# Cross-attention queries as three fp32r products, fewer keys and values ahead, and shorter norm and gate chains in a two-layer decoder

## The chip, the cores and the metric

The kernel runs on one core of a Trainium2 chip. The metric is the device time of one launch in microseconds. TensorE multiplies, VectorE (DVE), ScalarE (ACT) and GpSimd (POOL) do the elementwise work, and SyncE (SP) issues most transfers.

## The reference

Input x is 16 sequences of 128 tokens by 128 channels; ctx is a second input of the same shape. Six stages follow one another, each as x + stage(layernorm(x)):

```
x = x + self_attention_0(norm(x))          # 16 heads of 8, causal
x = x + cross_attention_0(norm(x), ctx)    # 8 heads of 64, plus a bias
x = x + ternary_ffn(norm(x))               # weights in {-1,0,1}, activations rounded to 8 bits
x = x + self_attention_1(norm(x))          # 16 heads of 8, causal, scores clipped to +-10
x = x + cross_attention_1(norm(x), ctx)    # 16 heads of 64
x = x + mixture(norm(x))                   # softmax gate over 8 experts, weights under 0.1 dropped, rest renormalised
```

The norm is (x - mean) / sqrt(var + 1e-5). The query of a cross attention is norm(x) @ Wq with Wq of 128 x 512 (first) or 128 x 1024 (second); its keys and values are ctx @ Wk and ctx @ Wv. All values are fp32.

## The kernel before

**Steps and orders.** The work of one sequence is cut into named steps (`all_steps`, line 55): `cross1.q.0` is the query projection of the first eight heads of the second cross attention, `.k` and `.v` its keys and values, `.s1` the scores, `.mx` the row maxima, `.ex` the exponentials, `.rc` and `.nz` the division by the sum, `.t` and `.wT` the transpose of the weights, `.pv` the product with the values, `.y` the output projection, `.res` the residual with the statistics of the next norm. Each step belongs to one engine. Steps of several sequences are interleaved: `ORDER` holds for every engine one long written-out string, two characters to a step, that gives the order in which that engine executes all steps of all 16 sequences. Every engine runs its string in order and waits at semaphores, so a late step holds up all behind it on its engine. The class `Plan` walks through the strings with the cost of each step and assigns the eight PSUM banks; TensorE then waits for the earlier user of a bank (`room`).

**Queries.** `four_pairs` (lines 1128 to 1133) makes a query step of four fp32 matmuls: stationary a 128x128 block of Wq, moving the transposed normalised input `xnT` of 128 columns. Each has its own column block of one PSUM bank, and ScalarE copies the bank to `qT`. cross0 has one such step for each sequence, cross1 two: 48 steps in all.

**Keys, values and experts** are already computed in three products. A matrix is split into a high part (ScalarE copies it to the type fp32r, line 803) and a low part (the difference, line 590 on DVE or GpSimd), and lo x hi, hi x lo and hi x hi are added up in PSUM. Keys are made for two sequences together, so 256 columns move (lines 1226 to 1228); values move 512 columns of weights (lines 1234 to 1236), experts too (lines 1334 to 1336). Keys and values depend on ctx alone, so their steps can be put anywhere; `AHEAD` gives the number of sequences for which they are kept, 8 for cross0 and 6 for cross1.

**Norm.** DVE computes mean and variance (`bn_stats`, `bn_aggr`, lines 891 to 893). GpSimd adds eps (line 665), drains, raises to the power -1/2 (line 667), drains and multiplies by the negated mean (line 669). ScalarE normalises (line 792), TensorE transposes (line 1360) and ScalarE copies to `xnT` (line 741). For the mixture ScalarE writes the transposed input twice (lines 808 and 809) and DVE takes its low part (line 906, step `moe.xl`). In the FFN DVE clamps the scaled units in PSUM (line 912), drains and rounds them (line 916).

**Gate.** After the exponentials with their sum, DVE takes the reciprocal of the sum (line 996), scales the eight exponentials twice (lines 998, 999), compares with 0.1 and keeps (line 1001), adds 1 where nothing is kept (line 1004), takes a reciprocal (line 1006) and scales (line 1010).

Of the kernel before, what the change touches and what calls it, by code (L numbers as in the profile page):

```python
# [6 lines left out]
F32 = mybir.dt.float32  # L7
# [24 lines left out]
AHEAD = dict(cross0=8, cross1=6)  # L32
# [32 lines left out]
def all_steps():  # L65
# [8 lines left out]
    def norm(L, source, users, read="xTe"):  # L74
        add(f"{L}.rs", "POOL", 1272, [source], [f"{L}.nm"])
# [5 lines left out]
        add(f"{L}.xTe", *(("DVE", 572) if L == "ffn" else ("ACT", 332 if L == "moe" else 166)), [f"{L}.xT"])  # L81
# [37 lines left out]
    def cross_attention(L, source, chunks, following, biased, k_w, v_w, loads):  # L119
# [15 lines left out]
        fill(f"{L}.y", 893 * chunks, [f"{L}.oTe.{c}" for c in range(chunks)], f"{L}.res")  # L135
# [6 lines left out]
    for name, load, engine, hi, lo in (("ctx0", "c0", "DVE", 530, 610), ("b_k", "b_k", "DVE", 530, 610),  # L142
                                       ("b_v", "b_v", "DVE", 530, 610), ("e_k", "e_k", "POOL", 960, 2390),
# [7 lines left out]
    cross_attention("cross0", "self0.res", 1, "ffn", ["self0.bi"], "b_k", "b_v", "in.more")  # L151
# [7 lines left out]
    cross_attention("cross1", "self1.res", 2, "moe", [], "e_k", "e_v", "in.cross1")  # L159
# [6 lines left out]
    add("moe.w", "DVE", 1650, ["moe.ex"], ["moe.ml", "moe.gT"])  # L166
# [24 lines left out]
        "aZaLbycubWbYa1bSaHcGbjbUaOblbCbabYaJcKbccybGaUbEbncBaQcqbWcCchb6bebJcjcsbwcacGb8byaXclccaZaLa4a1bQa6"
        "aHcubjaObCbSaJblbGbEcyaQbnb0aUcBcKbUbacqchbcbJcsbeaXbwb6cCcaaLbyaZb8aHa1clcjccbQb2cubScGbWbUcKbjbCaO"
        "blbabEb0aJbnbccyaQaUbGcBcCb6cqb8bebJcsaXchbwcaccaZbyaLcjclcGa4a1cua6aHbjbQaOblbaaJa4bncyaQbcbSaUbCcK"
        "cBbUchbEcCcqbebJcscjaXb6bwbWcGb8aZaLcabya1bGccclaHcubjbQbYaOblbSbCb2bUbEbaaQcybncKbcchb6bGcBaUcab8be"
        "bJcjbYcqcCclcccsaXcGbwcuaJaLbybjaZbQb0b0a1blaObCaHbnbSbEa6a6aQbGcyaJbYbUcKcBaUbacCbcchcqbwb6bebJaXb8"
        "cGbycaaLcjcsccaHaZcla1cubjbYb0aOblbQb2bnbaaUcybcaQcKcBbSchaJcqbUbeaXcGcCbCcjcsaOb6aZbGb0caa1aLb8bEcK"
        "aQccbwaUclbjbycuaXbYblbJaZbab2cya1bcbncBcqbecCbCbacsbQcGbYbcchbSbEbGcKbUbjcjbJbeblb6cub8bwcaccbybWcl"
        "cybnbQb2cBbjbWcCbCbSblbEbGbUchbncqbJb6cjbwcab8cGbyclcscccubQb0b2bwbWbCbSbWcybEcKbUbGcBchcCbycjbJb6cq"
        "cab8csccclbCcubEb0bQbJbGbSbYbUchb2cGcycjb6bYcBcacqb8clcsbQcKcccGbSb0bUcucCb6b2b8cacqchcccjclcycsb0b2"
        "cBcCcKcuchcqcjcGcycscBcKcucCcGcKcycBcCcGcK"  # L200
    ),
    DVE=(
        "aEaEarataEavaPaTbpbraEaYaTaPaEa2aYaEaPaTaEbfa2bhaYaTaPa2bfboaYaEbubhbxa2aTbzaPbfboaEbhaYbubKbNa2bfbx"
        "bzbhbRaTboaPbVbubKbNbxbfbzbocdbhaYcfbRcma2bVcobubNbKbxbzcdaEbocmbRaPbVcfbuaTcocvbxaEbfbzaYbKbNbha2cm"
        "cAcDcdcocFcIcvbRaTcfaPbVcLcDbocAcFbfbucIbKaEbNbhaYbxcmcdbRbzcva2cobVaTcLaPcAcfcDbocFaEcIbubfbNbKbxbh"
        "bzaYcmcda2bRcocvcfaPaTbocAcDcLbVbucFaEbKbNbfaYbxcIbha2cmbzcdbRcocvcLcfbVaPaTboaEcAcDcFcIbubfbNbKaYbx"
        "bhcdbzcma2cfcvcobRaPaTcAbocLcDbVcFcIbubfbNbKaYbxbhbzaEcda2cmcvcfbRaPbVaTcLcAcocDbocFbfbNbubKbhcIcmcd"
        "aYbxcvbzcfbRa2coaPboaTcAbVcLcDbucFcIbxbfbNbKbzbhaYcdcma2cvcfcoaTaPbRcAcLcDbocFbVbfaYcIbhbuaPa2aTcLbx"
        "cdcmbzcfcvaYcobKa2cAbNcDbobfcFbhbRcIbVbucLbNbfbKcvbxbhcdbzcmbobRcAcDcfcocFbVcIbobubKbNbxbzcmcdbucvbR"
        "cfbxcocLcAcDbVcFcIbzbKbNcdcmcvcfbRbKbVcobNcDcFcmbRcLcdcAbVcocfcIcvcdcmcfcAcDcocLcvcFcIcDcAcFcLcvcIcA"  # L210
        "cDcFcLcIcL"
    ),
# [16 lines left out]
    POOL=(
        "apaFaFaFaNaxaSaWazaFaBaNaWaSa8aFaDaNaFaSaWa3a8biaNaFaWa3aSbsa8a3bia8aNbAaFaWaSbsbIbiaNbMbPa3bAa8aFbi"  # L230
        "bsaWb4bIaSbMbAbPbsbicga8b4cpa3aNbIbPbMbsbAaFb4cgaScpaWcwbAa3bIbMbibPaNa8aFcpcwcJcgaWb4bsaSbIbMbPbicJ"
        "bAaNa8a3cwaFb4cpbIcgbsaSaWcJbPbMbia3bAaNa8cwcpa3aFcgbsaSb4aWbIbPbMcJbibAa8aNcwaFb4cpbsaSaWbIcgcJbMbi"
        "bPa3a8bAcgcwcpaFa3aNaSbsb4aWcJbPbibIbMbAa8cwcgaFb4bscpa3bIaNaSaWbibMbPcwbAcga8a3cJbsaScpb4aNaWcJbIbi"
        "bAaNbMbPa8cwcgcpaWaSb4bscJbiaNa8a3aSaWbIbAcwcpa8bMbPcgbsbicJb4bPa3cwa3bMbIbibAbscgcpb4cJbIbsbMbPbAcw"
        "cgcpb4bIbAcJbMbPcwcgbIb4cpbMbPb4cpcgcwcJcgcpcwcJcwcJcJ"
# [17 lines left out]
def switch(name):  # L253

    step = name.split(".")[1]
    return 150 if step in ("xT", "oT", "gT", "t") else 107 if step == "pv" and name[:4] == "self" else 196
# [80 lines left out]
class Stage:  # L337


    def __init__(self, nc, ctx, name):  # L340
        self.nc, self.ctx, self.name = nc, ctx, name
        self.moments = self.sb("moments", [P, 6])
        self.mean_var = self.sb("mean_var", [P, 2])
        self.var_eps = self.sb("var_eps", [P, 1])
# [14 lines left out]
class Attention(Stage):  # L359
    def __init__(self, nc, ctx, name, heads, units, width, chunks, maxima):  # L360
# [3 lines left out]
        self.xnT = sb("xnT", [P, P])  # L364
# [54 lines left out]
def decoder(nc, t, out):  # L419
    ctx = ExitStack()  # L420
    with ctx:
# [86 lines left out]
        wt["b_q"] = sb("b_q", [P, 8 * XD])  # L508
        wt["e_q"] = sb("e_q", [P, 16 * XD])
        for name, width in (("b_k", 8), ("b_v", 8), ("e_k", 16), ("e_v", 16)):  # L510
            wt[name], low[name] = twice(name, [P, width * XD])
# [226 lines left out]
        def _(act):  # L738
# [72 lines left out]
            def do_step(i, name, L, step, u):  # L811
# [6 lines left out]
                if step == "xTe":  # L818
# [609 lines left out]
```

## Time and profile before

| what | value |
|---|---|
| median of 3 runs | 508.68 us (508.4 to 509.6) |
| span of the profiled execution | 507.0 us |
| TensorE matmul busy | 492.5 us (97%) |
| TensorE weight load busy | 417.4 us (82%) |
| DVE busy | 411.2 us (81%) |
| ScalarE busy | 438.2 us (86%) |
| GpSimd busy | 390.3 us (77%) |
| mean granted clock of TensorE | 0.994 |

The span is from the first to the last instruction of one profiled execution; its own whole time stands in no row, and the median of the runs is 1.7 us above the span. Busy times of different engines overlap. A matmul's record reaches from its start to its modelled end, so records of consecutive matmuls overlap as well; their spacing shows in their starts. PEld is TensorE's weight load.

### The profile page before, as it was taken

Reading aid. Unit: us, or ns where it says so; the run is one execution under the profiler, and the core shown is the slowest. Engines: PE = TensorE matmul, PEld = TensorE weight load, DVE = VectorE, ACT = ScalarE, POOL = GpSimd, SP = SyncE. Lnnn points to the kernel's source line nnn. Section 1 sums busy time; section 2 is a strip of 40 time slices with the busy share of each in tenths; the row PEclk is TensorE's granted clock in tenths of the full one; section 3 lists DMA queues with packets and bytes.
Section 4 is the critical chain, followed back from the end, with each engine's and each line's share of the span. In section 5 each row is a group of like instructions: output and inputs, shape, how many; then the busy total and the mean of one; then the engine's idle time right before and its main releaser. Section 6 shows DMA issues by size and latency. Waiting matters only on the chain.

```text
span 507.0 us, 15965 instructions
## 1 busy us (share of the span) xinstructions
PE 492.5 (97%) x5508; PEld 417.4 (82%) x5508; DVE 411.2 (81%) x939; ACT 438.2 (86%) x1177; POOL 390.3 (77%) x553
## 2 busy tenths in 40 slices
PE   6999999999999999999999999999999999999994
PEld 3878887788888888889888888888988888888882
DVE  3867787887989888989898898888888788876665
ACT  4988889999999888998899998999889899898761
POOL 3787678787678689897798877988777788685663
PEclk8999999999999999999999999999999999999998
DMA  6800000000000000000000000000000000000000
GB/s 197 324 3 2 1 3 1 3 3 2 1 3 1 8 2 8 1 7 3 7 3 7 2 2 8 2 6 3 8 6 2 7 1 5 6 1 8 1 6 16
DMA packets 6462, 8.65 MB, mean 17 GB/s; under 512 B 1393, under 2 KB 4849, under 8 KB 6385
## 3 DMA queue, kind: packets, MB, share of 16 engines
q1 hardware_dynamic: 5952, 6.86, 4.1%
q8 instruction: 45, 0.74, 0.6%
q10 hardware_dynamic: 432, 0.79, 0.5%
q14 instruction: 33, 0.26, 0.2%
HBM read 6.50 MB, written 1.05 MB: 15 GB/s over the span
## 4 chain that ended last, share of the span: by engine, by line
PE 76%; DVE 9%; ACT 6%; issue 3%; DVEq 3%; POOL 1%; DMA 1%; POOLq 0%; SPq 0%; ACTq 0%
PE psum L1188 11%; PE psum L1215 8%; PE psum L1243 8%; PE psum L1175 8%; PE psum L1131 7%; PE psum L1162 5%; ACT w_cross L776 3%; PE psum L1201 2%; PE psum L1360 2%; PE psum L1254 2%; PE psum L1234 2%; PE psum L1226 2%; PE psum L1228 2%; PE psum L1227 2%; PE psum L1236 2%
## 5 line engine op out<-in xcount | busy, mean ns | idle before, releaser
L694 POOL TENSOR_TENSOR w_self<-w_self 128x1024 f16<-128x1024 f32 x64 | 120.9, 1899 | 13.8 <-ACT w_self L759 9.9
L776 ACT ACTIVATE w_cross<-psum,row_max_cross 128x128 f32<-128x128 f32 x384 | 104.5, 405 | 6.8 <-DVE row_max_cross L922 6.2
L699 POOL TENSOR_TENSOR w_cross<-w_cross,e_rec_cross 128x1024 f32<-128x1024 f32 x48 | 91.0, 1899 | 10.3 <-DVE e_rec_cross L931 9.7
L922 DVE TENSOR_REDUCE row_max_cross<-psum 128x8 f32<-128x1024 f32 x48 | 58.0, 1214 | 9.9 <-PE psum L1175 9.5
L929 DVE TENSOR_REDUCE e_sum_cross<-w_cross 128x8 f32<-128x1024 f32 x48 | 58.3, 1215 | 1.8 <-ACT w_cross L776 1.7
L1175 PE MATMUL psum<-kT_cross,qT_cross 64*128 64x128 f32 x768 | 54.2, 283 | 0.0
L1215 PEld LDWEIGHTS psum<-w_cross,v_cross 128*64 128x64 f32 x768 | 41.2, 136 | 15.3 <-issue 13.0
L784 ACT ACTIVATE w_cross<-psum 128x1024 f32<-128x1024 f32 x48 | 50.0, 1048 | 3.2 <-PE psum L1188 3.2
L1215 PE MATMUL psum<-w_cross,v_cross 128*64 128x128 f32 x768 | 51.4, 278 | 0.9 <-ACT w_cross L784 0.6
L1175 PEld LDWEIGHTS psum<-kT_cross,qT_cross 64*128 64x128 f32 x768 | 46.2, 187 | 6.9 <-issue 4.8
L1188 PE MATMUL psum<-ident,w_cross 128*128 128x128 f32 x384 | 49.5, 274 | 0.8 <-POOL w_cross L699 0.8
L1188 PEld LDWEIGHTS psum<-ident,w_cross 128*128 128x128 f32 x384 | 43.0, 142 | 2.2 <-issue 1.0
L938 DVE TENSOR_REDUCE row_max_self<-psum 128x8 f32<-128x1024 f32 x32 | 39.0, 1219 | 3.0 <-PE psum L1162 2.6
L940 DVE TENSOR_TENSOR w_self<-psum,row_max_self 128x1024 f32<-128x1024 f32 x32 | 39.2, 1225 | 2.4
L759 ACT ACTIVATE w_self<-w_self,shift 128x1024 f32<-128x1024 f32 x32 | 37.0, 1167 | 2.1 <-DVE w_self L949 2.1
L949 DVE SCALAR_TENSOR_TENSOR w_self<-psum,s_bound 128x1024 f32<-128x1024 f32 x32 | 38.0, 1215 | 0.3 <-PE psum L1162 0.3
L741 ACT ACTIVATE by_head_self<-psum,head_mask 128x128 f32<-128x128 f32 x128 | 37.7, 415 | 0.0
L1162 PE MATMUL psum<-by_head_self,plain_self 32*128 32x512 f32 x256 | 37.2, 651 | 0.4 <-ACT w_cross L776 0.2
L741 ACT ACTIVATE attnT_cross<-psum 128x512 f32<-128x512 f32 x48 | 30.1, 632 | 6.4 <-PE psum L1215 6.2
L765 ACT ACTIVATE w_self<-psum 128x1024 f32<-128x1024 f32 x32 | 33.4, 1042 | 2.6 <-PE psum L1188 2.4
L741 ACT ACTIVATE qT_cross<-psum 128x512 f32<-128x512 f32 x48 | 29.2, 614 | 6.1 <-PE psum L1131 4.7
L1188 PE MATMUL psum<-ident,w_self 128*128 128x128 f32 x256 | 33.5, 274 | 0.3 <-DVE w_self L940 0.3
(198 smaller groups left out, 1412.5 us busy)
## 6 DMA issues: line engine op xcount, KB each, us to landing
out_dram<-x_all SPq DMA_DIRECT2D x16, 64.0 KB, 1.5
x_all<-in_x SPq DMA_DIRECT2D x1, 768.0 KB, 7.0
cT_all<-in_ctx SPq DMA_DIRECT2D x1, 768.0 KB, 9.0
e_k<-in_e_k SPq DMA_DIRECT2D x1, 512.0 KB, 4.7
e_v<-in_e_v SPq DMA_DIRECT2D x1, 512.0 KB, 5.6
e_q<-in_e_q SPq DMA_DIRECT2D x1, 512.0 KB, 8.9
e_o<-in_e_o SPq DMA_DIRECT2D x1, 512.0 KB, 9.7
m_w<-in_m_w SPq DMA_DIRECT2D x1, 512.0 KB, 9.0
```

The lines of the kernel that those rows point to most:

```text
L694: pool.tensor_tensor(L.w_low[u], L.w[u][:], halves(L.w[u][:]), ALU.subtract)\
L699: pool.tensor_tensor(L.diff[u][:].rearrange("p (h k) -> p h k", h=UNIT), L.e[u][:].rearrange("p (h k) -> p h k", h=UNIT), L.e_rec[:, u, :] ...
L741: act.activation(dst, src, ACT.Copy, **scale).then_inc(emptied(i, name)[0], 1)
L776: last = act.activation(L.e[u][:, P * p:P * (p + 1)], S_[:, P * p:P * (p + 1)], ACT.Exp, bias=L.row_max[:, u, p:p + 1])
L784: act.activation(L.w[u][:], group(i, turn)[:], ACT.Copy).then_inc(taken(i, turn)[0], 1)
L922: dve.tensor_reduce(L.row_max[:, u, :], group(i, turn)[:].rearrange("p (h k) -> p h k", h=UNIT), AX_X, ALU.max, negate=True).then_inc(L.ma ...
L929: dve.tensor_reduce(L.e_sum[:, u, :], L.e[u][:].rearrange("p (h k) -> p h k", h=UNIT), AX_X, ALU.add)
L1162: last = pe.matmul(group(i, name, u)[:, 512 * half:512 * (half + 1)], L.plain[rows, :], L.by_head[rows, :, :].rearrange("p j n -> p (j n)" ...
L1175: last = pe.matmul(S_[:, at:at + P], L.qT[rows, h // 2, :], kT[rows, h // 2, i % 2, :], start=True, stop=True)
L1188: last = pe.transpose(S_[:, P * k:P * (k + 1)], L.diff[u][:, P * k:P * (k + 1)], ident[:])
L1215: last = pe.matmul(bank(i, name)[rows, P * pair:P * (pair + 1)], v[:, h, :], L.w[c][:, P * place(h):P * (place(h) + 1)], start=True, stop= ...
L1243: last = pe.matmul(bank(i, name)[:, 0:P], L.attnT[:, c, :], w(c), start=c == 0, stop=c == n - 1)
```

## The change

The query step becomes twelve fp32r matmuls. `xnT` of the cross attentions is replaced by `xn_hi` (ScalarE) and `xn_lo` (DVE, a new step `xl` between transpose and query), and b_q and e_q are split into parts once. The low part takes the place of the loaded weights, the high part is new memory; `AHEAD` of cross0 goes from 8 to 6. The variance gets its eps from a third, constant group of moments (zero count and mean, 128 x 1e-5 as its sum of squares), so line 665 goes. The FFN clamp goes. The gate compares the exponentials with 0.1 times their sum and divides once, by the kept sum. All four `ORDER` strings are new, with other costs in the plan (query 893 to 700, norm on GpSimd 1272 to 940). The array's partition changes 191 times in TensorE's old order and 200 times in the new one.

```diff
-AHEAD = dict(cross0=8, cross1=6)
+AHEAD = dict(cross0=6, cross1=6)
@@ all_steps, cross_attention
-        norm(L, source, [f"{L}.q.{c}" for c in range(chunks)])
+        norm(L, source, [f"{L}.q.{c}" for c in range(chunks)], "xl")
+        add(f"{L}.xl", "DVE", 215, [f"{L}.xTe"])
         for c in range(chunks):
-            fill(f"{L}.q.{c}", 893, [f"{L}.xTe", loads], f"{L}.qe.{c}", [f"{L}.s1.{c}"])
+            fill(f"{L}.q.{c}", 700, [f"{L}.xl", f"{q_w}.lo"], f"{L}.qe.{c}", [f"{L}.s1.{c}"])
@@ rstd (GpSimd)
-                pool.tensor_tensor(L.var_eps[:], L.mean_var[:, 1:2], eps[:], ALU.add)
-                pool.drain()
-                pool.tensor_tensor(L.rstd[:], L.var_eps[:], minus_half[:], ALU.pow)
+                pool.tensor_tensor(L.rstd[:], L.mean_var[:, 1:2], minus_half[:], ALU.pow)
@@ ScalarE
+            def high_query(L, i):
+                act.wait_ge(x_full, full(i, f"{L.name}.xT"))
+                act.activation(L.xn_hi[:], bank(i, f"{L.name}.xT")[:, 0:P], ACT.Copy).then_inc(L.high_ready, 1)
@@ DVE
-                dve.bn_stats(L.moments[:], x)
+                dve.bn_stats(L.moments[:, 0:6], x)
+            def low_query(L, i):
+                dve.wait_ge(L.high_ready, i + 1)
+                dve.tensor_tensor(L.xn_lo[:], bank(i, f"{L.name}.xT")[:, 0:P], L.xn_hi[:].bitcast(F32), ALU.subtract)\
+                    .then_inc(emptied(i, f"{L.name}.xT")[0], 1)
-                dve.tensor_scalar(units, units, Q_MAX, -Q_MAX - 1, ALU.min, ALU.max)
@@ gate_weights (DVE)
-                dve.reciprocal(g_rec[:], g_sum[:])
-                dve.drain()
-                dve.tensor_scalar(g_soft[:], gates(i, 1), g_rec[:], None, ALU.mult)
-                dve.tensor_scalar(gates(i, 2), gates(i, 1), g_rec[:], None, ALU.mult)
+                dve.tensor_copy(g_exp[:], gates(i, 1))
+                dve.tensor_scalar(g_least[:], g_sum[:], THRESHOLD, None, ALU.mult)
                 dve.drain()
-                dve.scalar_tensor_tensor(out=gates(i, 3), in0=gates(i, 2), scalar=THRESHOLD, in1=g_soft[:],
+                dve.scalar_tensor_tensor(out=gates(i, 2), in0=gates(i, 1), scalar=g_least[:], in1=g_exp[:],
                                          op0=ALU.is_ge, op1=ALU.mult, accum_out=g_keptsum[:])
                 dve.drain()
-                dve.tensor_scalar(g_guarded[:], g_keptsum[:], 0.0, g_keptsum[:], ALU.is_equal, ALU.add)
-                dve.drain()
-                dve.reciprocal(g_rec2[:], g_guarded[:])
+                dve.reciprocal(g_rec[:], g_keptsum[:])
@@ DVE, before the constants are announced
+            for L in stages.values():
+                dve.memset(L.moments[:, 6:8], 0.0)
+                dve.memset(L.moments[:, 8:9], P * LN_EPS)
@@ TensorE
-            def four_pairs(i, name, w, c, xT):
+            def queries(L, i, name, c):
+                hi, lo = high[f"{L.letter}_q"], low[f"{L.letter}_q"]
                 for k in range(4):
-                    col = P * (4 * c + k)
-                    last = pe.matmul(bank(i, name)[:, P * k:P * (k + 1)], w[:, col:col + P], xT,
-                                     start=True, stop=True)
+                    block, out_ = slice(P * (4 * c + k), P * (4 * c + k + 1)), bank(i, name)[:, P * k:P * (k + 1)]
+                    pe.matmul(out_, lo[:, block], L.xn_hi[:], start=True, stop=False)
+                    pe.matmul(out_, hi[:, block], L.xn_lo[:], start=False, stop=False)
+                    last = pe.matmul(out_, hi[:, block], L.xn_hi[:], start=False, stop=True)
                 last.then_inc(x_full, 1)
@@ cross_step (TensorE), step q: at i == 0 it waits for the low part of its weights; the wait for the loads moves to step y
...
```

## Rows read from the trace of the kernel before

**Rows 1.** The page's head and busy times; busy tenths of TensorE in 40 slices.
```profile
span 507.0 us, 15965 instructions
PE 492.5 (97%) x5508; PEld 417.4 (82%) x5508; DVE 411.2 (81%) x939; ACT 438.2 (86%) x1177; POOL 390.3 (77%) x553
...
PE   6999999999999999999999999999999999999994
```

**Rows 2.** The chain that ended last, share of the span by engine and by line.
```profile
PE 76%; DVE 9%; ACT 6%; issue 3%; DVEq 3%; POOL 1%; DMA 1%; POOLq 0%; SPq 0%; ACTq 0%
...
by line: PE psum L1188 11.5%; PE psum L1215 8.4%; PE psum L1243 8.1%; PE psum L1175 8.0%; PE psum L1131 7.1%; PE psum L1162 5.2%; ACT w_cross L776 3.2%; issue 3.2%; PE psum L1201 2.5%; PE psum L1360 2.4%; PE psum L1254 2.0%; PE psum L1234 1
```

**Rows 3.** Busy us by stretch: length, PE, PEld, DVE, ACT, POOL, clock, DMA, GB/s.
```profile
250.00:300.00 50.00, 50.00 (x621) 43.23 (x620) 43.65 (x101) 45.49 (x124) 44.36 (x60) 1.00 0.01 4
...
400.00:450.00 50.00, 49.88 (x548) 42.99 (x545) 40.09 (x99) 45.64 (x122) 39.55 (x60) 1.00 0.02 4
```

**Rows 4.** L1131 over the span (PE, PEld busy); then one group by form.
```profile
0.00:507.00 507.00, 50.56 (x384) 46.51 (x384) 0.99 0.05 17
...
L1228 PEld LDWEIGHTS psum<-cT_hi,e_k_hi 128*128 128x128 f32 x64 | 12.1, 189 | 0.0
```

**Rows 5.** The chain in order of time, 50 to 80 us: start, us, what.
```profile
53.67 0.89 PE psum L1131 x8
...
58.43 1.09 PE psum L1175 x16
```

**Rows 6.** TensorE's timeline, key steps of cross1: start, us; two of seven.
```profile
20.08 0.28 PE L1226 MATMUL psum<-cT_hi,e_k_lo 128*128 128x256 f32 x1
...
20.80 0.28 PE L1226 MATMUL psum<-cT_hi,e_k_lo 128*128 128x256 f32 x1
```

**Rows 7.** Timeline of weight loads (PEld) and one matmul, in three places.
```profile
128.15 0.19 PEld L1226 LDWEIGHTS psum<-cT_hi,e_k_lo 128*128 128x128 f32 x1 [0.76 <-issue]
...
128.26 0.19 PEld L1227 LDWEIGHTS psum<-cT_all_lo,e_k_hi 128*128 128x128 f32 x1
...
128.38 0.28 PE L1227 MATMUL psum<-cT_all_lo,e_k_hi 128*128 128x256 f32 x1
128.38 0.19 PEld L1228 LDWEIGHTS psum<-cT_hi,e_k_hi 128*128 128x128 f32 x1
...
150.05 0.19 PEld L1334 LDWEIGHTS psum<-m_w_hi,moe_lo 128*128 128x128 f32 x1
...
150.17 0.19 PEld L1335 LDWEIGHTS psum<-m_w_lo,moe_hi 128*128 128x128 f32 x1
...
204.42 0.10 PEld L1203 LDWEIGHTS psum<-v_self,w_self 128*128 128x128 f16 x1
204.45 0.10 PEld L1201 LDWEIGHTS psum<-v_self,w_self 128*128 128x128 bf16 x1
```

**Rows 8.** Groups by form: busy us, mean ns of one, idle before.
```profile
L922 DVE TENSOR_REDUCE row_max_cross<-psum 128x8 f32<-128x1024 f32 x48 | 58.0, 1214 | 9.9 <-PE psum L1175 9.5 <-issue 0.2
...
L912 DVE TENSOR_SCALAR psum<-psum 128x128 f32<-128x128 f32 x16 | 4.6, 290 | 0.7 <-PE psum L1360 0.6
...
L906 DVE TENSOR_TENSOR moe_lo<-psum,moe_hi 128x128 fp32r<-128x128 f32 x16 | 4.4, 274 | 1.4 <-ACT moe_hi L809 1.4
...
L665 POOL TENSOR_TENSOR var_eps_cross<-mean_var_cross,eps 128x1 f32<-128x1 f32 x32 | 6.1, 191 | 10.9 <-DVE mean_var_cross L893 10.4
...
L590 POOL TENSOR_TENSOR e_k_lo<-e_k,e_k_hi 128x1024 fp32r<-128x1024 f32 x1 | 2.4, 2404 | 2.8 <-ACT e_k_hi L803 2.8
```

**Rows 9.** DVE's timeline, the last sequence's gate: start, us.
```profile
499.05 0.16 DVE L996 RECIPROCAL g_rec<-g_sum 128x1 f32<-128x1 f32 x1 [0.46 <-ACT psum L871]
499.29 0.23 DVE L998 TENSOR_SCALAR g_soft<-psum,g_rec 128x8 f32<-128x8 f32 x1
...
500.04 0.21 DVE L1004 TENSOR_SCALAR g_guarded<-g_keptsum 128x1 f32<-128x1 f32 x1
...
500.33 0.16 DVE L1006 RECIPROCAL g_rec<-g_guarded 128x1 f32<-128x1 f32 x1
```

More of the change, by code:

```diff
@@ L74, in norm @@
     def norm(L, source, users, read="xTe"):
-        add(f"{L}.rs", "POOL", 1272, [source], [f"{L}.nm"])
+        add(f"{L}.rs", "POOL", 940, [source], [f"{L}.nm"])
         add(f"{L}.nm", "ACT", 380, [f"{L}.rs"], [f"{L}.un" if L == "ffn" else f"{L}.xT"])
@@ L80, in norm @@
         fill(f"{L}.xT", 109, [f"{L}.un" if L == "ffn" else f"{L}.nm"], f"{L}.{read}", users)
-        add(f"{L}.xTe", *(("DVE", 572) if L == "ffn" else ("ACT", 332 if L == "moe" else 166)), [f"{L}.xT"])
+        add(f"{L}.xTe", *(("DVE", 250) if L == "ffn" else ("ACT", 332 if L == "moe" else 166)), [f"{L}.xT"])
     def self_attention(L, source, maxima, following, loads, loads_out):
@@ L134, in cross_attention @@
             add(f"{L}.oTe.{c}", "ACT", 486, [f"{L}.pv.{c}"])
-        fill(f"{L}.y", 893 * chunks, [f"{L}.oTe.{c}" for c in range(chunks)], f"{L}.res")
+        fill(f"{L}.y", 893 * chunks, [*(f"{L}.oTe.{c}" for c in range(chunks)), "in.more" if L == "cross0" else "in.cross1"], f"{L}.res")
         add(f"{L}.res", "DVE", 840, [f"{L}.y", *biased], [f"{following}.rs"])
@@ L142, in all_steps @@
     for name, load, engine, hi, lo in (("ctx0", "c0", "DVE", 530, 610), ("b_k", "b_k", "DVE", 530, 610),
-                                       ("b_v", "b_v", "DVE", 530, 610), ("e_k", "e_k", "POOL", 960, 2390),
+                                       ("b_v", "b_v", "DVE", 530, 610), ("b_q", "more", "DVE", 530, 610),
+                                       ("e_q", "cross1", "POOL", 960, 2370), ("e_k", "e_k", "POOL", 960, 2390),
                                        ("e_v", "e_v", "POOL", 960, 2370), ("ctx1", "ctx", "POOL", 1400, 3510),
@@ L150, in all_steps @@
     add("self0.bi", "POOL", 412, ["self0.res", "in.more"], [ago("cross0.res", 2)])
-    cross_attention("cross0", "self0.res", 1, "ffn", ["self0.bi"], "b_k", "b_v", "in.more")
+    cross_attention("cross0", "self0.res", 1, "ffn", ["self0.bi"], "b_q", "b_k", "b_v")
     add("tern.abs", "DVE", 300, ["in.more"], once=True)
@@ L158, in all_steps @@
     self_attention("self1", "ffn.res", False, "cross1", "in.self1", "in.self1")
-    cross_attention("cross1", "self1.res", 2, "moe", [], "e_k", "e_v", "in.cross1")
+    cross_attention("cross1", "self1.res", 2, "moe", [], "e_q", "e_k", "e_v")
     norm("moe", "cross1.res", ["moe.g", "moe.e"], "xl")
@@ L165, in all_steps @@
     add("moe.ex", "ACT", 279, ["moe.lg"])
-    add("moe.w", "DVE", 1650, ["moe.ex"], ["moe.ml", "moe.gT"])
+    add("moe.w", "DVE", 1240, ["moe.ex"], ["moe.ml", "moe.gT"])
     fill("moe.gT", 110, ["moe.w"], "moe.gTe", ["moe.b"])
@@ L191 @@
[L191 to L195, printed above, removed]
@@ new lines @@
+        "b9aRaWbNbRbFbUbnbxcmaJb9a7bca7cvbUbNbRaRbxaHbFcmcvaWb9a0aJbFcCbNaRbcbnbRbUcPaJcCcma0b9bNbxcvaWbRbUcP"
+        "bna7cCbcbFb9aRcvaJa7bxcmaWa0bNcPbUbnbRbFcCa7bcaRcvcmbxaWb9a0bNbUbRbFaJbncPcCbcaRcvcmb9aWbxa0cPbRbNbn"
+        "bUcCa7bcbFaRcmcvbxaWa0b9a7aJcPbUbNbnbRbFcCbccmaRb9a7aWbxaJbNcva0bUbnbRcCbFbccPcvbxaJcmb9aRa0aWcPbRaR"
+        "bnbNbUa7bccCbFcma0a7cvbxaWb9cPbnaWaRa0bcbFcmcCcvbNbRbcbUbxbncPb9bNbUcCbRbna7a7bFcmcvbxb9bxcPbNbRbUbF"
+        "cCcmcvb9bFcPbNbRbUcCcmbNb9cvbRbUb9cvcmcCcPcmcvcCcPcCcPcP"
@@ L255, in switch @@
     step = name.split(".")[1]
-    return 150 if step in ("xT", "oT", "gT", "t") else 107 if step == "pv" and name[:4] == "self" else 196
+    if step == "pv":
+        return 107 if name[:4] == "self" else 147
+    return 150 if step in ("xT", "oT", "gT", "t") else 196
 class Plan:
@@ L341, in __init__ @@
         self.nc, self.ctx, self.name = nc, ctx, name
-        self.moments = self.sb("moments", [P, 6])
+        self.moments = self.sb("moments", [P, 9])
         self.mean_var = self.sb("mean_var", [P, 2])
-        self.var_eps = self.sb("var_eps", [P, 1])
         self.minus_mean = self.sb("minus_mean", [P, 1])
@@ L378, in __init__ @@
         Attention.__init__(self, nc, ctx, name, SH, 2, SD, 1, maxima)
+        self.xnT = self.sb("xnT", [P, P])
         self.v = self.sb("v", [P, SH, 3, SD + 1])
@@ L392, in __init__ @@
         Attention.__init__(self, nc, ctx, name, heads, heads // UNIT, XD, heads // UNIT, True)
+        self.xn_hi = self.sb("xn_hi", [P, P], F32R)
+        self.xn_lo = self.sb("xn_lo", [P, P], F32R)
+        self.high_ready = self.sem("high_ready")
         self.v = [self.sb(f"v{b}", [P, heads, XD]) for b in range(AHEAD[name])]
@@ L507, in decoder @@
         low = {}
-        wt["b_q"] = sb("b_q", [P, 8 * XD])
-        wt["e_q"] = sb("e_q", [P, 16 * XD])
-        for name, width in (("b_k", 8), ("b_v", 8), ("e_k", 16), ("e_v", 16)):
+        for name, width in (("b_q", 8), ("e_q", 16), ("b_k", 8), ("b_v", 8), ("e_k", 16), ("e_v", 16)):
             wt[name], low[name] = twice(name, [P, width * XD])
@@ L527, in decoder @@
         cross0.letter, cross1.letter = "b", "e"
-        cross0.q_w, cross0.k_w, cross0.v_w, cross0.o_w = (wt[x] for x in ("b_q", "b_k", "b_v", "b_o"))
-        cross1.q_w, cross1.k_w, cross1.v_w, cross1.o_w = (wt[x] for x in ("e_q", "e_k", "e_v", "e_o"))
+        cross0.o_w, cross1.o_w = wt["b_o"], wt["e_o"]
         a_max = sb("a_max", [P, 1])
@@ L568, in decoder @@
         moe_high = sem("moe_high")
-        CUT = dict(ctx0="c0", b_k="b_k", b_v="b_v", e_k="e_k", e_v="e_v", ctx1="ctx", m_w="moe")
+        CUT = dict(ctx0="c0", b_k="b_k", b_v="b_v", b_q="more", e_q="cross1", e_k="e_k", e_v="e_v", ctx1="ctx", m_w="moe")
         hi_ready = {name: sem(f"hi_ready_{name}") for name in CUT}
@@ L827, in do_step @@
                         moe_parts(i)
+                    elif L in (cross0, cross1):
+                        high_query(L, i)
                     else:
@@ L1055, in do_step @@
                     low_part(dve, name.partition(".")[0])
-                if step == "xl":
+                if step == "xl" and L is moe:
                     moe_low(i)
+                if step == "xl" and L is not moe:
+                    low_query(L, i)
                 if step == "st":
@@ L1292, in cross_step @@
                     if i == 0:
-                        load = "more" if L is cross0 else "cross1"
-                        pe.wait_ge(loaded[load], load_count(load))
+                        pe.wait_ge(lo_ready[f"{L.letter}_q"], 1)
                     pe.wait_ge(*emptied(i, f"{L.name}.xT"))
                     room(i, name)
-                    four_pairs(i, name, L.q_w, u, L.xnT[:])
+                    queries(L, i, name, u)
                 if step == "s1":
@@ L1302, in cross_step @@
                 if step == "y":
+                    if i == 0:
+                        load = "more" if L is cross0 else "cross1"
+                        pe.wait_ge(loaded[load], load_count(load))
                     project(L, i, name, 4 * L.chunks, lambda c: L.o_w[:, c, :])
```

89 lines of the change are left out of this document (43 added, 46 removed).

## The prediction

> **What bounds the kernel now.** I read the page's head first. The span is 507.0 us; TensorE is busy for 492.5 us of it and shows nine tenths or more in every slice but the first and the last [rows 1]. A busy TensorE is not proof of a bound, because the modelled end of a matmul reaches over gaps, so the second view is the chain of waits: 76% of it runs on TensorE, DVE has 9%, ScalarE 6% and GpSimd 1% [rows 2]. The third view, busy time by stretches, shows the other engines with room in the middle of the run: of 50 us ScalarE works 45 to 46, DVE 40 to 44, GpSimd 40 to 44, while TensorE works 50 at the full clock [rows 3]. So the time is that of TensorE's written order. What the change does to the length of a TensorE step is paid nearly in full; what it takes from the other engines is worth something only at the two ends.
>
> **The queries, which are the heart of the change.** A query step is now four fp32 matmuls of 128x128 by 128x128, and each is recorded as two weight loads and two matmuls: 384 records of each kind, 48 steps of eight [rows 4]. On the chain one step of eight records takes 0.89 us, so a record takes 0.111 us [rows 5]. After the change a step is twelve fp32r matmuls over 128 moving columns, each with its own weight load: 576 loads and matmuls instead of 384.
>
> What does one of them take? No fp32r matmul of 128 columns is in the trace, so I bound it. The streaming of the columns alone: six fp32r matmuls of 256 columns start 0.72 us apart, 0.12 us each [rows 6], so 128 columns would stream in 0.06 us if nothing else limited them. The load of the weights: at 128.15 a load of fp32r weights starts on a TensorE that had been waiting, and the next load starts 0.11 us later; at 150.05, behind matmuls of only 8 columns (L1321), the next one starts 0.12 us later. The two-byte loads of the self attention follow each other in 0.03 to 0.05 us with the same 128x128 shape [rows 7]. The load for the next matmul starts together with the matmul before it (L1227's matmul and L1228's load, both at 128.38), so a pair takes the longer of load and stream. Keys (256 columns) hide a load of 0.11 us under a stream of about the same length, and values (512 columns) do so with room to spare; 128 columns can't. So a pair takes 0.111 to 0.12 us, the load, and I take 0.111, the fp32 row of the same shapes, because the 0.12 is from rows in which 256 columns stream.
> Step after: 12 x 0.111 = 1.33 us (1.44 at 0.12). Step before: 0.89 us. Longer by 0.44 us (0.55). Over 48 steps: +21.3 us (up to +26).
> From the other side, if the stream were the limit, 12 x 0.06 = 0.72 us, shorter by 0.17 us, over 48 steps -8.3 us. If fp32r over few columns took the array as long as fp32 does (two records of 0.111 us for a product), a step would take 12 x 0.222 = 2.66 us, over 48 steps +85 us; nothing in the rows speaks for it.
>
> The third product has the same stationary block as the second, as it has in the key step. That doesn't save a load: L1228, which is that third product, runs twice in each of cross1's 32 key steps and has 64 loads [rows 4].
>
> A page of the Trainium skill bears on this. "TensorE: Matmul & The Clock Gate", section "Weight-path perf modes", says that a faster weight load is on when 128 weights are loaded and their type is not fp32. If fp32r counted as "not fp32" there, the load would vanish and the step would take the 0.72 us above; the trace disagrees, since its fp32r loads keep the spacing of fp32 ones and not that of the two-byte ones [rows 7].
>
> How much reaches the end: the chain gives L1131 7.1% of 507.0 us [rows 2], 36.0 us out of 384 x 0.111 = 42.6 us, so 84% of the query time lies on it. That path is there again in a like order, which makes +17.9 us of the +21.3. The other 16% also holds up a serial engine, but TensorE has idle moments to put it in. I take +19.5, half way.
>
> **The other edits.**
> - Norm chains: one GpSimd add of 0.19 us and its drain go from each of 96 norms [rows 8]. GpSimd holds 1% of the chain, 5 us, and the add is about a fifth of a norm's GpSimd work: -1 us at most on the chain, the rest is hidden by TensorE.
> - FFN clamp: one DVE operation of 0.29 us sixteen times, 4.6 us of DVE; added is the low part of the normalised input, 32 operations of 0.27 us as L906 has them, 8.8 us [rows 8]. Net 4 us more over the run, on an engine with 6 to 10 us of room in each 50. The low part also stands between transpose and query: ScalarE's copy, then 0.27 us of DVE. What hides it is that other sequences' steps stand between xT and q in TensorE's order; where DVE is in the middle of a 1.2 us reduction (L922) the query, and all TensorE work queued behind it, can be held up to 1.5 us. Such cases are in my upper end (+2 us), and my value for them is +0.5 us.
> - Gate: in the last sequence its DVE chain runs bare from 499.05 us on [rows 9]. Gone are a reciprocal, two scalings and the guard; a copy, a scaled threshold and one reciprocal stay in their place. From the first reciprocal's start to the next instruction's it is 0.24 us, for the guard 0.29 us: together -0.5 us, and this one is paid out in full.
> - Splitting b_q and e_q: a copy of each on ScalarE, a subtraction of 2.4 us on GpSimd for e_q, as for e_k of its size [rows 8], and one of half the elements on DVE for b_q; once and early. The first query waits for them, yet its step is late in the order and key and value steps stand before it: 0, at most +1 us. SP's and ScalarE's DMA queues keep their order. The twelve memsets of two or fewer columns before `consts` stand where DVE next waits for x0 to land: 0, or their own short length if that landing comes first.
> - Keys and values of cross0 6 ahead, not 8: the order written out before has at most 7 such steps outstanding, the new one 6. These are TensorE's filler; with the engine late at every query no filler is missed: 0.
> - The new order changes the array's partition 200 times against 191. A change costs some 0.1 to 0.2 us of TensorE: the 16 records of an L1175 step, which run in pairs on two halves of the array, take 1.09 us with the change, and eight at 0.111 would be 0.89 [rows 5]. Nine changes at 0.1: +0.9 us (+1.8).
> Sum: 507.0 + 19.5 - 1 + 0.5 - 0.5 + 0.9 = 526.4 us of span. The median of the runs, 508.68, lies 1.7 us above the span of the profiled execution, so 528.1; I round to 528.
>
> **Rivals.**
> A. The new query step streams at 0.06 us a product. Time: 507.0 - 8.3 x 0.84 - 1 + 0.5 - 0.5 + 0.9 + 1.7 = 501.6, faster by 1.4%. For it: twelve times 128 columns are as many columns as a key or value step has, and these take 0.7 us [rows 6]. Against it: the loads of rows 7. It is the case on the other side; it decides once a load of fp32r weights takes under 0.07 us (12 x 0.07 = 0.84, below 0.89).
> B. The step is longer, but much is absorbed. Idle time of TensorE and 24% of the chain off it leave places; with a third of the load hidden or two thirds of the lateness absorbed, +4 to +9 us: 511 to 519. Against it: 84% of the query time is on the chain. To this case belongs also that product three keeps product two's weights (8 loads at 0.111 and 4 streams at 0.06 make 1.13 us a step, +11.4 us, 519), which L1228's count speaks against.
> C. fp32r over 128 columns is as slow as fp32: +85 us, 590. Nothing in the rows shows it; nothing at 128 columns excludes it.
> D. The change has no effect: only if a pair takes 0.074 us, between both bounds by luck.
> The same page of the Trainium skill, section "Back-to-back issue gap", gives 81 ns for each pair of load and matmul in a sustained stream of 128 columns. By that figure a query step would take 0.97 us, an estimate, and the whole change about +3 to +4 us, in the low part of B; the fp32 and fp32r rows here show 0.11 us, while two-byte pairs over fewer columns run faster.
>
> **How the numbers follow.** Forecast (load-bound, nearly all paid) 0.74, own range 522 to 535: the low end is +17.9 with all savings and a tight order, the high end 0.12 us a pair on the chain (+22) with stalls of the longer chain (+3). B 0.09 (509 to 521), A 0.12, C 0.03, D 0.02. From 510 to 535 leaves out A, C, D and the tails of the forecast, about 2 in 10. A measurement of this kernel can tell 0.3%, or 1.5 us, from no change. Slower by more than that: 0.74 + 0.09 + 0.03 = 0.86 with a little of B lost, 0.85; within it 0.03; faster 0.12.
>
> **What would show it.** In the changed trace: the query line with 576 loads and 576 matmuls; starts of its matmuls 0.11 us apart and a step of 1.33 us on the chain; the page's share of that line in the chain at 10 to 12% instead of 7%; TensorE busy in nine tenths of every slice as before; ScalarE's and DVE's shares down by some 3% of the span since their work hardly changes; the last gate chain 0.5 us shorter. Starts 0.06 us apart would prove A. Starts 0.11 us apart with a span under 519 would prove B, and then the waits of TensorE should have shrunk by the difference. The prediction is wrong if the load of fp32r weights depends on something that keys, values and experts don't show.

## The result, and the profile after

The changed kernel takes 531.91 us (median of 5 runs, 531.03 to 532.56) against 508.80 us of the kernel before on the same chip: ratio 1.045, 95% interval 1.0431 to 1.0469, slower by 23 us. The forecast was 528 with a range of 510 to 535.

The page's head, which answers to [rows 1]:

```profile
span 530.8 us, 16121 instructions
PE 514.5 (97%) x5700; PEld 439.8 (83%) x5700; DVE 411.5 (78%) x936; ACT 442.9 (83%) x1179; POOL 375.1 (71%) x458
PE   7999999999999999999999999999999999999994
```

TensorE has 192 instructions more of each kind (576 - 384) and is as full as before; ScalarE went from 86% to 83%, DVE from 81% to 78%, GpSimd from 77% to 71%. The span grew by 23.8 us, TensorE's busy time by 22.0. The chain of waits, by engine and by line ([rows 2]):

```profile
PE 79%; POOL 6%; ACT 5%; issue 4%; DVE 3%; POOLq 2%; DMA 1%; DVEq 0%; ACTq 0%
...
by line: PE psum L1203 11.5%; PE psum L1190 9.0%; PE psum L1230 8.0%; PE psum L1258 7.7%; PE psum L1177 5.5%; PE psum L1145 3.9%; PE psum L1147 3.9%; PE psum L1146 3.9%; issue 3.8%; PE psum L1216 2.6%; PE psum L1377 2.6%; PE psum L1269 2.4%
```

The three query lines L1145 to L1147 now have 11.7% of 530.8 us, 62 us, where L1131 had 36 us. TensorE's timeline shows a query step of cross1, start and us, the first five of twelve:

```profile
299.98 0.31 PE L1145 MATMUL psum<-xn_hi_cross,e_q_lo 128*128 128x128 f32 x1
300.12 0.27 PE L1146 MATMUL psum<-xn_lo_cross,e_q_hi 128*128 128x128 f32 x1
300.23 0.27 PE L1147 MATMUL psum<-xn_hi_cross,e_q_hi 128*128 128x128 f32 x1
300.34 0.28 PE L1145 MATMUL psum<-xn_hi_cross,e_q_lo 128*128 128x128 f32 x1
300.45 0.28 PE L1146 MATMUL psum<-xn_lo_cross,e_q_hi 128*128 128x128 f32 x1
```

After the first, a start each 0.11 us, so twelve take 1.33 us: the spacing of the loads in [rows 7], not half that of the 256-column products in [rows 6]. And each product loads its own weights, also the third, whose block is that of the second. Groups by form of the loads, of the new low part on the way to the query, and of GpSimd's power (L667), with which the norm chain on GpSimd begins now that L665 is gone:

```profile
L1145 PEld LDWEIGHTS psum<-xn_hi_cross,e_q_lo 128*128 128x128 f32 x128 | 24.6, 192 | 2.1 <-DVE xn_lo_cross L917 1.1 <-issue 0.8
L1146 PEld LDWEIGHTS psum<-xn_lo_cross,e_q_hi 128*128 128x128 f32 x128 | 24.5, 192 | 0.0
L1147 PEld LDWEIGHTS psum<-xn_hi_cross,e_q_hi 128*128 128x128 f32 x128 | 24.6, 192 | 0.0
L917 DVE TENSOR_TENSOR xn_lo_cross<-psum,xn_hi_cross 128x128 fp32r<-128x128 f32 x32 | 8.9, 278 | 4.2 <-ACT xn_hi_cross L807 3.9
L667 POOL TENSOR_TENSOR rstd_cross<-mean_var_cross,minus_half 128x1 f32<-128x1 f32 x32 | 18.0, 562 | 14.9 <-DVE mean_var_cross L899 14.7
```

The last gate chain on DVE, which answers to [rows 9]:

```profile
523.45 0.17 DVE L1007 COPY g_exp<-psum 128x8 f32<-128x8 f32 x1 [0.26 <-ACT psum L877]
...
524.36 0.23 DVE L1017 TENSOR_SCALAR g_weight<-psum,g_rec 128x8 f32<-128x8 f32 x1
524.50 0.28 DVE L1039 TENSOR_TENSOR x_all<-psum,weighted 128x128 f32<-128x128 f32 x1
524.93 1.22 DVE L1025 TENSOR_TENSOR weighted<-psum,g_weight 128x1024 f32<-128x1024 f32 x1
```

From its first instruction to x_all (L1039, the residual sum of the sequence before) it takes 1.05 us. Before, it was 1.66, from 499.05 in [rows 9] to the same step at 500.71.

### The profile page after: what moved, and what is told of

The parts are those of the page before. It is cut to its first block, busy times and chain, and to the rows that moved or that the text cites. A ratio compares the mean times of both kernels' runs of the same rounds, so it can differ in the third digit from the quotient of the medians.

```text
span 530.8 us, 16121 instructions
## 1 busy us (share of the span) xinstructions
PE 514.5 (97%) x5700; PEld 439.8 (83%) x5700; DVE 411.5 (78%) x936; ACT 442.9 (83%) x1179; POOL 375.1 (71%) x458
## 3 DMA queue, kind: packets, MB, share of 16 engines
HBM read 6.50 MB, written 1.05 MB: 14 GB/s over the span
## 4 chain that ended last, share of the span: by engine, by line
PE 79%; POOL 6%; ACT 5%; issue 4%; DVE 3%; POOLq 2%; DMA 1%; DVEq 0%; ACTq 0%
PE psum L1203 11%; PE psum L1190 9%; PE psum L1230 8%; PE psum L1258 8%; PE psum L1177 6%; PE psum L1145 4%; PE psum L1147 4%; PE psum L1146 4%; PE psum L1216 3%; PE psum L1377 3%; PE psum L1269 2%; POOL w_self L694 2%; ACT w_cross L776 2%; PE psum L1218 2%; PE psum L1249 1%
## 5 line engine op out<-in xcount | busy, mean ns | idle before, releaser
L1145 PE MATMUL psum<-xn_hi_cross,e_q_lo 128*128 128x128 f32 x128 | 36.0, 281 | 0.5 <-DVE xn_lo_cross L917 0.5
L1147 PE MATMUL psum<-xn_hi_cross,e_q_hi 128*128 128x128 f32 x128 | 35.3, 275 | 0.0
```

Of the source, the lines that this page charges most:

```text
L1145: pe.matmul(out_, lo[:, block], L.xn_hi[:], start=True, stop=False)
L1147: last = pe.matmul(out_, hi[:, block], L.xn_hi[:], start=False, stop=True)
```

## The experiments

Each ratio below is to the kernel before on the same chip, with its 95% interval.

**The queries alone undone** (q_fp32).

```diff
-                    pe.matmul(out_, lo[:, block], L.xn_hi[:], start=True, stop=False)
-                    pe.matmul(out_, hi[:, block], L.xn_lo[:], start=False, stop=False)
-                    last = pe.matmul(out_, hi[:, block], L.xn_hi[:], start=False, stop=True)
+                    last = pe.matmul(out_, w[:, block], L.xnT[:], start=True, stop=True)
... xnT instead of xn_hi and xn_lo; b_q and e_q unsplit; step xl empty
```

> The changed kernel with the queries alone undone: four fp32 matmuls on an unsplit b_q and e_q, no low part of the input; new order, cross0 6 ahead, short norm and gate chains stay. Theory 1 (the 12 weight loads of 0.111 us are the price, 48 x 0.44 = 21.3 us): 510 to 512 us. Rival 2 (a good part comes from the new order, the array's 9 more partition changes, or 6 ahead): 515 to 525. Rival 3 (the short chains hide a gain that the queries eat): under 507.

Measured: 510.81 us, ratio 1.0027 (1.0011 to 1.0043). The queries carry 1.045 - 1.0027 = 4.2% of 508.8 us, 21.5 us, give or take 1.3 by the two intervals; theory 1 had 21.3.

**Half the columns** (q_half).

```diff
-                    pe.matmul(out_, lo[:, block], L.xn_hi[:], start=True, stop=False)
+                    half = out_[:, 0:P // 2]
+                    pe.matmul(half, lo[:, block], L.xn_hi[:, 0:P // 2], start=True, stop=False)
... the other two products in the same way
```

> The changed kernel with only the first 64 of the 128 columns moving in each of the 12 query matmuls (half of the queries are left out of the computation); the weight loads are the same 12. Theory 1 (load-bound): unchanged, 531 to 532.5 us, starts still 0.11 us apart. Rival 4 (the columns of fp32r are what takes 0.111 us, so few of them are streamed slowly): starts 0.055 us apart, a step of 0.67 us, 48 x 0.66 = 32 us less at most, 500 to 506 us.

Measured: 534.92 us, ratio 1.0526 (1.0475 to 1.0578). Its timeline of TensorE, a query step of cross1:

```profile
180.79 0.28 PE L1146 MATMUL psum<-xn_hi_cross,e_q_lo 128*128 128x64 f32 x1
180.91 0.28 PE L1147 MATMUL psum<-xn_lo_cross,e_q_hi 128*128 128x64 f32 x1
181.02 0.28 PE L1148 MATMUL psum<-xn_hi_cross,e_q_hi 128*128 128x64 f32 x1
181.13 0.28 PE L1146 MATMUL psum<-xn_hi_cross,e_q_lo 128*128 128x64 f32 x1
```

Half the columns, the same 0.11 us: the columns aren't what is waited for, and rival 4 is out. Theory 1 missed the time all the same, by 2.4 us above its upper end. Busy us by stretch (length, PE, PEld, DVE, ACT, POOL, clock):

```profile
200.00:210.00 10.00, 10.00 (x105) 8.52 (x105) 7.85 (x23) 7.87 (x22) 8.03 (x8) 1.00 0.03 9
210.00:220.00 10.00, 10.00 (x115) 9.67 (x114) 7.32 (x14) 7.10 (x17) 8.37 (x9) 0.83 0.01 2
...
360.00:370.00 10.00, 10.00 (x113) 9.03 (x109) 6.03 (x11) 7.11 (x19) 8.76 (x11) 0.71 0.01 2
```

The granted clock falls below full in places, so part of these stretches ran at 1.2 instead of 2.4 GHz, although TensorE's record shows no idle time in them. The changed kernel has 1.00 in all its stretches from 25 to 500 us. The timeline of TensorE where the clock falls, at 364 us:

```profile
363.98 0.28 PE L1148 MATMUL psum<-xn_hi_cross,e_q_hi 128*128 128x64 f32 x1
364.09 0.29 PE L1146 MATMUL psum<-xn_hi_cross,e_q_lo 128*128 128x64 f32 x1
364.20 0.40 PE L1147 MATMUL psum<-xn_lo_cross,e_q_hi 128*128 128x64 f32 x1
364.41 0.40 PE L1148 MATMUL psum<-xn_hi_cross,e_q_hi 128*128 128x64 f32 x1
364.62 0.40 PE L1146 MATMUL psum<-xn_hi_cross,e_q_lo 128*128 128x64 f32 x1
```

At the lower level the same products start 0.21 us apart instead of 0.11, so a pair takes about twice as long there. Just before, TensorE had done 19 products of 64 columns since 361.81, and before the fall at 214 us it had done 24 of them from 210.80 to 213.56. In this one execution the clock can account for the whole lateness: if work at half the clock takes twice as long, a mean clock of 0.978 over 538.2 us costs 11.8 us, and the changed kernel's 0.994 over 530.8 us costs 3.2, an estimate of 8.7 us more for a span that is 7.4 us longer. It can't account for all of it in the others: of the four executions one had 0.994 as well and took 534.3 us, where the changed kernel took 532.56 at 0.994. Those 1.7 us, 1.1 when each is set against the kernel before as measured with it (509.44 and 508.80), stay open.

**Three loads for the same columns** (q_swap).

```diff
-                for k in range(4):
-                    ... 3 matmuls of a 128x128 block of the weights by 128 columns of the input
+                w = slice(512 * c, 512 * (c + 1))
+                pe.matmul(bank(i, name)[:], L.xn_hi[:], lo[:, w], start=True, stop=False)
+                pe.matmul(bank(i, name)[:], L.xn_lo[:], hi[:, w], start=False, stop=False)
+                last = pe.matmul(bank(i, name)[:], L.xn_hi[:], hi[:, w], start=False, stop=True)
```

> The changed kernel with the roles of the operands swapped in the query step, as in the value step: the input's high and low parts are stationary and 512 columns of the weights move, so 3 loads and 3 x 512 columns in place of 12 loads and 12 x 128 (queries come out untransposed and all that follows is computed from the wrong layout). Theory 1: a step takes 3 x 0.233 = 0.70 us, 48 x 0.63 = 30 us less, of which 85 to 100% reach the end: 501.5 to 506 us. Rival 5 (other engines bound the kernel as soon as TensorE gets shorter): 507 to 512. Rival 4 (columns, not loads): unchanged at 532, since the same 1536 columns stream.

Measured: 503.67 us, ratio 0.9885 (0.9858 to 0.9912). A step of cross1 in its timeline:

```profile
100.59 0.50 PE L1144 MATMUL psum<-e_q_lo,xn_hi_cross 128*128 128x512 f32 x1
100.92 0.39 PE L1145 MATMUL psum<-e_q_hi,xn_lo_cross 128*128 128x512 f32 x1
101.15 0.40 PE L1146 MATMUL psum<-e_q_hi,xn_hi_cross 128*128 128x512 f32 x1
```

The second and third start 0.23 us apart. The same 1536 columns with a quarter of the loads save 1.045 - 0.9885 = 5.65%, 28.7 us of the 30 possible, so the other engines would have let TensorE's gain through (rival 5 is out). It is also the price of rival A in the forecast, 501.6, had the loads been free. It is no version to use: the queries come out with tokens and channels exchanged.

**Two of the three products** (two_products).

```diff
-                    pe.matmul(out_, lo[:, block], L.xn_hi[:], start=True, stop=False)
-                    pe.matmul(out_, hi[:, block], L.xn_lo[:], start=False, stop=False)
+                    pe.matmul(out_, hi[:, block], L.xn_lo[:], start=True, stop=False)
                     last = pe.matmul(out_, hi[:, block], L.xn_hi[:], start=False, stop=True)
```

> The changed kernel with two of the three products in each query block (the product of the weights' low part is left out of the computation): 8 loads and 8 matmuls in place of 12. Theory 1 (each load of fp32r weights costs 0.111 us): step 0.89 us, the time of q_fp32 or up to 1 us above it for the low part on DVE, ratio to before 1.002 to 1.006. Rival 9 (a third or more of the price is not in the loads but in the longer way over DVE and the start of a group): ratio over 1.012.

Measured: 510.81 us, ratio 1.0032 (1.0017 to 1.0048). Eight loads of fp32r cost what eight halves of fp32 cost, and the longer way over DVE adds 0.0005 against q_fp32, nothing that can be told.

**The three products in the first cross attention alone** (cross0_only): fp32 queries for cross1, e_q unsplit, otherwise the changed kernel.

```diff
+                if L is cross1:
+                    ... four fp32 matmuls of wt["e_q"] by L.xnT, as before
                 hi, lo = high[f"{L.letter}_q"], low[f"{L.letter}_q"]
```

> The changed kernel with three products for the queries of cross0 alone, fp32 queries for cross1: 16 long steps instead of 48. Theory 1 (price in proportion to the steps): a third of the way from q_fp32 (1.0027) to the changed kernel (1.045), ratio 1.015 to 1.019. Rival 10 (the price is in the second cross attention, whose two query steps stand close together and whose chain is long): under 1.010. Rival 9: over 1.025.

Measured: 518.18 us, ratio 1.017 (1.0152 to 1.0189). A third of the steps, a third of the price: 1.0027 + 0.0423 / 3 = 1.0168.

**The short chains alone, in the kernel before** (chains_only).

```diff
-                pool.tensor_tensor(L.var_eps[:], L.mean_var[:, 1:2], eps[:], ALU.add)
... the diffs of the norm, the clamp and the gate; orders, queries and 8 ahead as before
```

> The kernel before, with its orders and fp32 queries, and only the short norm, gate and clamp chains (no eps add, eps in a third group of moments; one reciprocal in the gate; no clamp). Theory 1 as predicted: 0.5 us of the last gate chain and up to 1 us of norm chains, ratio to before 0.997 to 0.999, and so the new order with cross0 6 ahead is what made q_fp32 0.3% slower. Rival 7 (the chains are worth more, 3 us or over, and the new order loses it all): ratio under 0.994. Rival 8 (shorter chains are fully hidden): ratio 1.000.

Measured: 506.18 us, ratio 0.9937 (0.9921 to 0.9954): more than theory 1 had, and just inside rival 7's range (under 0.994), though its interval reaches past it. It is the fastest here of the versions that compute all that the reference asks for, 3.2 us below the kernel before. Its last gate chain:

```profile
498.24 0.17 DVE L991 COPY g_exp<-psum 128x8 f32<-128x8 f32 x1 [0.46 <-ACT psum L867]
...
499.29 0.28 DVE L1023 TENSOR_TENSOR x_all<-psum,weighted 128x128 f32<-128x128 f32 x1
499.71 1.22 DVE L1009 TENSOR_TENSOR weighted<-psum,g_weight 128x1024 f32<-128x1024 f32 x1
```

1.05 us, 0.6 shorter than before. The rest lies earlier, and was split:

**The norm chain alone** (norm_only: only line 665 and its drain go, with the third group of moments) and **gate and clamp alone** (gate_clamp_only).

> The kernel before with the short norm chain alone (96 GpSimd adds of 0.19 us and their drains gone). The three short chains together gave a ratio of 0.9937, 3.2 us. Theory 13 (the norm chain is on the way at many places of the 16 sequences, so it carries most): 0.995 to 0.997, and gate and clamp alone 0.998 to 0.999. Theory 1 as predicted (1 us at most from the norms): 0.998 to 1.000.

> The kernel before with the short gate chain and without the FFN clamp, norms as before. Its last gate chain runs bare, and the trace of the three together has it 0.6 us shorter. Theory 13: 0.998 to 0.999. Rival 14 (the clamp, in front of the FFN's product in every sequence, carries the rest): 0.995 to 0.997.

Measured: 0.9953 (0.9936 to 0.9971) and 0.9959 (0.9947 to 0.9971). Theory 13 holds for the norms (2.4 us), not for gate and clamp (2.1 us), whose ratio is the one that rival 14 expected. Which of gate and clamp carries how much wasn't tried; the last gate's 0.6 us is the part that a trace shows. Of the norm chain the trace of the kernel before shows what went: besides L665's 0.19 us [rows 8], L667 waited 4.6 us in 32 norms after it, 0.14 us each.

```profile
L667 POOL TENSOR_TENSOR rstd_cross<-var_eps_cross,minus_half 128x1 f32<-128x1 f32 x32 | 17.6, 551 | 4.6 <-issue 0.2
```

The two ratios multiply to 0.9912, below the 0.9937 of all three together, but the intervals overlap.

**The plan's cost of a query step** (plan_1330: changed kernel; q_fp32_plan893: q_fp32; before_plan700: kernel before). The orders stay. Only the PSUM banks that the plan picks change.

```diff
-            fill(f"{L}.q.{c}", 700, ...
+            fill(f"{L}.q.{c}", 1330, ...
```

> The changed kernel with the plan's cost of a query step at 1330 instead of 700 ns; the orders stay, only the choice of PSUM banks changes (309 of 721 steps get other banks). Theory 1 (TensorE's length decides, banks hardly stall it): 531 to 532.5 us. Rival 6 (banks chosen by too short a query step make TensorE wait): 524 to 529.

> q_fp32 with the plan's query cost at 893 ns, what such a step takes, instead of 700: only PSUM banks change. The plan with 1330 made the changed kernel slower by 8 us, so the choice of banks has a price of its own. Rival 11 (a plan with costs that fit gives better banks): ratio under 1.0027, towards 1.000. Rival 12 (the orders were searched together with the banks that cost 700 gives, and any other choice is worse): ratio 1.006 or over. Theory 1 says nothing of it but that TensorE's weight loads are the same in both.

> The kernel before with nothing changed but the plan's cost of a query step, 700 instead of 893 ns, which here is too low: 98 of 721 steps get other banks. Rival 11 and rival 12 both expect it slower, ratio 1.004 to 1.012; a ratio of 1.000 would say that banks matter only in the new orders.

Measured: plan_1330 539.65 us, ratio 1.0595 (1.0565 to 1.0626), 7.4 us over the changed kernel; q_fp32_plan893 520.10 us, 1.0209 (1.019 to 1.0229), 9.3 us over q_fp32; before_plan700 511.91 us, 1.0046 (1.0031 to 1.0062). My first expectation, that banks hardly stall TensorE, was wrong. The page's busy times of q_fp32 and of q_fp32_plan893:

```profile
span 509.2 us, 15701 instructions
PE 493.6 (97%) x5508; PEld 419.0 (82%) x5508; DVE 403.0 (79%) x903; ACT 438.9 (86%) x1177; POOL 371.8 (73%) x457
```

```profile
span 516.8 us, 15705 instructions
PE 493.0 (95%) x5508; PEld 418.0 (81%) x5508; DVE 403.8 (78%) x903; ACT 439.4 (85%) x1177; POOL 371.3 (72%) x457
```

The same work in the same order, and TensorE idle for 23.8 us instead of 15.6. TensorE's waits in the second (us, times, longest):

```profile
PE psum L1191 <- ACT w_cross L777: 1.7, 2, 1.2
PE psum L1149 <- ACT w_cross L777: 1.5, 2, 0.8
...
PE psum L1149 <- ACT kT_cross L742: 1.3, 2, 1.1
```

These are waits for ScalarE's reads out of PSUM, of exponentials (L777) and keys, and of them L1149, which writes the mask at the start of the first self attention's scores, needs nothing of them but their bank. None of the three is among q_fp32's six longest. Together they are 4.5 us, against 8.2 us that TensorE is idle longer; the rest is spread over other waits.

**The short chains with fitting costs** (chains_plan: chains_only with norm 940, clamp and rounding 250, gate 1240 in the plan).

> The three short chains in the kernel before, and the plan told of them (norm 940, clamp and rounding 250, gate 1240 ns): 67 of 721 steps get other banks, the orders stay. Rival 11 (fitting costs give better banks): below 0.9937. Rival 12 (the orders were searched with the banks of the old costs, another choice is worse, as in both cases so far): 0.998 to 1.005, in proportion to the 67 steps (271 other steps cost 1.8% in the q_fp32 pair).

Measured: 508.61 us, 0.997 (0.9959 to 0.9982), so half of the gain is lost. Rival 11 falls a second time, after q_fp32_plan893, and rival 6, which expected the same of plan_1330, had fallen too. Better costs gave worse banks in q_fp32 and here, and a worse cost too in before_plan700. Rival 12 agrees with all four in sign; its size is missed in chains_plan, 0.997 against 0.998 to 1.005. That the orders were searched together with their banks is an inference; the runs show only that any other choice tried was slower.

## Why the prediction was right

- **What bounds the kernel.** Right. TensorE's order set the time, and q_swap shows that it would have done so downwards too.
- **The query step.** Right in mechanism and size: 1.33 us for twelve products, load-bound, with 576 loads. q_half took the columns away and left the spacing, q_swap took the loads away and left the columns; two_products and cross0_only show the price in proportion to loads and to steps.
- **How much reaches the end.** I took +19.5 of 21.3 us; the runs give 21.5 (q_fp32 against the changed kernel). The 16% of query time off the old chain was paid as well. The chain after has the three lines for 62 us of 576 x 0.111 = 64 us, 97% and not 84%. The 84% belonged to one path among several of nearly the same length: with the same 384 query records the chain gives the query line 8.1% of 505.6 us in chains_only, 41 us, and 8.6% of 509.2 us in q_fp32, 44 us, no less than the 42.6 us of query time.
- **Order and partition changes.** Sized at +0.9 us; it is q_fp32 against chains_only, 1.0027 - 0.9937 = 0.9%, 4.6 us, five times as much. The two differ in the order, its banks and 6 or 8 ahead; I had counted switches and not asked what banks do. In one profile of each, TensorE is busy for 493.6 against 492.4 us and idle for 15.6 against 13.2, so about a third of the difference is longer work and the rest is waiting. How it divides among order, banks and 6 ahead wasn't tried. This is the largest miss in the sum.
- **Short chains.** Sized at -1.5 us together, measured -3.2 in the old order, from norms and from gate and clamp in like parts. I had taken GpSimd's 1% of the chain as the limit of what its instructions are worth. What left each norm was 0.33 us, the add and the wait behind it, 32 us over the 96 norms, and 2.4 of them reached the end. What such an instruction delays can be booked by the chain on another engine: in the changed kernel the chain gives GpSimd 6%, although its busy time fell by 15 us. That this is the reason is argued, not shown. The last gate chain's part (0.5 predicted, 0.6 found) was paid in full: in both kernels L1018 or L1025 follows x_all by 0.42 to 0.43 us. The rest was mis-sized.
- **The low part on DVE.** +0.5 us predicted; two_products against q_fp32 shows +0.0005 of the time, 0.3 us, within noise.
- **The sum.** In ratios: queries +4.23%, order +0.90%, chains -0.63%, together +4.50% and 22.9 us, against 20.0 (with the low part's 0.5) + 0.9 - 1.5 = 19.4 expected. The misses, +1.5, +3.7 and -1.7 us, partly cancelled; that the time came within 4 us of 528 is in part owed to this.
- **Rivals.** A (free loads) would have been 501.6; q_swap measured 503.7 for its condition. B fell with the 21.5 us paid, C with the spacing of 0.11 us, D with the ratio. The Trainium skill, "TensorE: Matmul & The Clock Gate", section "Back-to-back issue gap", has 81 ns for a pair of load and matmul at 128 columns. That doesn't hold for fp32r here, where 111 ns was measured. The same page of the Trainium skill, section "Weight-path perf modes", has a fast weight load for types other than fp32. It doesn't show on fp32r weights in this trace: their loads start 0.11 us apart, two-byte ones 0.03 [rows 7].

## What to carry to other kernels

Before splitting an fp32 matmul into three fp32r products, count weight loads, not columns: a load of 128 columns of fp32r weights took 0.11 us. With 128 moving columns three products take 0.33 us and one fp32 matmul 0.22. With 256 they take 3 x 0.12 = 0.36 us [rows 6] against 0.44 for fp32 in two matmuls of 128, an estimate, since no trace here has fp32 over 256 columns on the whole array; so the split can pay from there on. Read a load's length where nothing else can hide it: behind an idle engine or behind tiny matmuls. And in a kernel with a written order, treat the assignment of PSUM banks as a part of the tuning that any change of a cost model can lose.

## What the hardware showed that was not expected

- With 64 moving columns in each load-bound product the granted clock fell to 0.83 and 0.71 in stretches of 10 us in which TensorE's record shows no gap (q_half), and the kernel was slower than with 128 columns, 1.0526 against 1.045. At the lower of the two levels the load-bound products start 0.21 us apart instead of 0.11.
- The choice of PSUM banks alone, with every instruction in its place, moved the time by 0.5% (98 of 721 steps, before_plan700), 0.3% (67 steps, chains_plan against chains_only), 1.4% (309 steps, plan_1330) and 1.8% (271 steps, q_fp32_plan893).
